# Shared experts first and a later routing step in two dense mixtures of a fused two-layer kernel

## The reference, cut to what matters

```python
shared = silu(h @ sWg) * (h @ sWu) @ sWd            # two shared experts' worth, width 256
routing_weights = sigmoid(h @ gate_w.T)             # 16 experts
topk_w, topk_idx = top_k(routing_weights, 8)
topk_w = topk_w / (sum(topk_w) + 1e-06) * 2.5
comb = zeros((T, 16)).at[arange(T)[:, None], topk_idx].add(topk_w)
eo[e] = (silu(h @ Wg[e]) * (h @ Wu[e])) @ Wd[e]     # every expert on every token
x = x + shared + sum_e eo[e] * comb[:, e]
```

## Time and profile before

| | |
|---|---|
| median of three runs | 1830.96 us |
| the profiled execution, its own time | 1826.19 us |
| its span, first to last instruction | 1824.3 us |
| PE busy | 1656.0 us, 91% |
| VectorE busy | 1331.1 us, 73% |
| ScalarE busy | 1009.8 us, 55% |
| GpSimd busy | 656.8 us, 36% |
| mean granted TensorE clock | 0.975 |
| HBM traffic over the span | 60 GB/s |

### The profile page before, as it was taken

The page is one execution under the profiler, slowest core; times in us unless marked ns, Lnnn a source line. Parts: engine busy times, 40 slices in busy tenths (PEclk is TensorE's granted clock), DMA queues, the critical chain, the costliest instruction groups (busy, mean ns, idle before and its releaser), DMA issues.

```text
span 1824.3 us, 34290 instructions
## 1 busy us (share of the span) xinstructions
PE 1656.0 (91%) x10911; PEld 1335.9 (73%) x10912; DVE 1331.1 (73%) x2842; ACT 1009.8 (55%) x2163; POOL 656.8 (36%) x604
## 2 busy tenths in 40 slices
PE   3877999899999999989999989899799999999998
PEld 1223888677777978777777779777588888887776
DVE  7997777778876577678778756665688888857664
ACT  4655543578786454348778744311588788744111
POOL 1664420266664042016566540100355555421000
PEclk8998999999999999999999999999899999999999
DMA  1000210000000122000000033398100010043695
GB/s 64 1 1 24 81 61 1 13 18 20 20 12 9 45 82 67 1 13 24 21 17 23 4 119 103 101 257 244 45 29 29 27 31 23 0 127 96 187 258 150
DMA packets 34895, 111.51 MB, mean 61 GB/s; under 512 B 4992, under 2 KB 18544, under 8 KB 27888
## 3 DMA queue, kind: packets, MB, share of 16 engines
q1 hardware_dynamic: 32424, 92.96, 16.8%
q10 hardware_dynamic: 2376, 17.30, 3.5%
HBM read 109.19 MB, written 1.05 MB: 60 GB/s over the span
## 4 chain that ended last, share of the span: by engine, by line
PE 65%; DVE 20%; ACT 8%; issue 6%; ACTq 1%; DMA 0%; DVEq 0%; POOL 0%; SPq 0%; POOLq 0%
PE banks L1046 8%; PE banks L1022 4%; PE banks L1762 4%; PE banks L1698 3%; PE banks L1001 3%; PE banks L594 3%; PE banks L596 3%; PE banks L595 3%; PE banks L1002 2%; PE banks L1003 2%; PE banks L953 2%; PE banks L1060 2%; PE banks L955 2%; PE banks L954 2%; PE banks L1061 2%
## 5 line engine op out<-in xcount | busy, mean ns | idle before, releaser
L1475 POOL TENSOR_TENSOR xn<-xn 128x512 f32<-128x512 f32 x132 | 171.4, 1299 | 247.5 <-DVE xn L1359 247.5
L1461 POOL TENSOR_SCALAR prob<-prob,recip 128x256 f32<-128x256 f32 (+2 forms) x256 | 228.5, 907 | 68.9 <-DVE recip L1343 68.8
L1230 ACT ACTIVATE prob<-banks,peak 128x256 f32<-128x256 f32 (+3 forms) x384 | 190.3, 501 | 107.7 <-DVE peak L1334 97.5
L1046 PE MATMUL banks<-pt,v 128*128 128x256 f32 (+3 forms) x768 | 203.2, 407 | 6.9 <-ACT pt L1165 6.9
L1046 PEld LDWEIGHTS banks<-pt,v 128*128 128x128 f32 x768 | 143.6, 189 | 73.5 <-issue 33.0
L1334 DVE TENSOR_REDUCE peak<-banks 128x1 f32<-128x256 f32 (+3 forms) x384 | 161.4, 448 | 16.6 <-PE banks L1005 15.2
L1001 PE MATMUL banks<-k_hi,q_hi 128*128 128x256 f32 (+2 forms) x384 | 152.2, 396 | 22.7 <-DVE k_lo L1350 22.4
L1446 POOL TENSOR_TENSOR wq_lo<-wq,wq_hi 128x256 fp32r<-128x256 f32 x48 | 35.7, 743 | 326.2 <-ACT wq_hi L1180 326.2
L1022 PE MATMUL banks<-ident,prob 128*128 128x128 f32 x864 | 140.6, 279 | 3.2 <-DVE pt L1163 3.2
L1359 DVE TENSOR_TENSOR xn<-xn,ropes 128x512 f32<-128x512 f32 x138 | 123.9, 898 | 0.0
L1002 PE MATMUL banks<-k_lo,q_hi 128*128 128x256 f32 (+2 forms) x384 | 120.4, 314 | 0.0
(11 more groups left out here) (255 smaller groups left out, 4988.2 us busy)
## 6 DMA issues: line engine op xcount, KB each, us to landing
wgu<-in_w_gu SPq DMA_DIRECT2D x32, 1408.0 KB, 15.0
wd<-in_w_d ACTq DMA_DIRECT2D x24, 704.0 KB
raw<-in_w SPq DMA_DIRECT2D x36, 384.0 KB, 3.1
wd<-in_w_d SPq DMA_DIRECT2D x8, 704.0 KB
wkv<-in_mha_kv SPq DMA_DIRECT2D x16, 256.0 KB, 2.6
wq<-in_mqa_q SPq DMA_DIRECT2D x16, 128.0 KB, 2.0
wo<-in_mqa_o SPq DMA_DIRECT2D x16, 128.0 KB, 2.1
wq<-in_gqa_q SPq DMA_DIRECT2D x16, 128.0 KB, 2.0
```

The costliest lines, as they stand in the source:

```text
L1046: last = pe.matmul(o_bank[:, x * P:to], v[:, s, x, at:at + P], pt[:, s, x, first:first + to - x * P], start=(j == 0), stop=(j == NQ - 1))
L1230: last = act.activation(prob[:, s, cols[t]:cols[t] + n], s_bank[gi][:, psum_col[t]:psum_col[t] + n], ACT.Exp, bias=peak[:, s, t:t + 1], ac ...
L1461: last = pool.tensor_scalar(part, part, recip[:, s, t:t + 1], None, ALU.mult)
L1475: pool.tensor_tensor(cosed_at(i, m, r), cosed_at(i, m, r), swap[:, r % 2, :], ALU.add) \
```

## The change

The expert that unit u computes is now `expert(u) = (u + 16) % 18`: the two shared experts come first, the routed ones behind. SP's loads and the column of the weights in `add` follow that order. `logits(0)` moves on PE from ahead of gate_up(0) to between gate_up(1) and down(0). DVE, after inner_low(0), waits for the logits and copies them raw from bank 6 to SBUF (count `shelved`); PE waits for that copy, not for the sigmoid, ahead of down(1). ACT's `gates(0)` now reads the copy in SBUF, in place, and moves behind inner_hi(1); the load of the sigmoid's table ahead of it is no longer written out, and a load of the silu's table follows it. `route(0)` moves on DVE from ahead of product(1) to behind add(1), ahead of product(3). The second sequence's logits, sigmoid and routing stay where they were. Both dense mixtures are built by the same function, so both change.

```diff
+    def expert(n):
+        return (n + NE0) % NU0
...
-            sp.dma_start(raw[:, n % 4, :], d["w0"][n]).then_inc(full[n % 4].sem, 16)
+            sp.dma_start(raw[:, n % 4, :], d["w0"][expert(n)]).then_inc(full[n % 4].sem, 16)
...
-        logits(0)
         norm.wait_parts(pe, 0)
         gate_up(0)
...
                 gate_up(u + 1)
+            if u == 0:
+                logits(0)
             if u == 1:
-                pe.wait_ge(c["gates"].sem, 1)
+                pe.wait_ge(c["shelved"].sem, 1)
...
         def gates(s):
-            act.wait_ge(c["logits"].sem, s + 1)
-            act.activation(score[:, s * HALF:(s + 1) * HALF, :].rearrange("p t e -> p (t e)"),
-                           g.banks[:, 6 - 2 * s, 0:HALF * NE0], ACT.Sigmoid).then_inc(c["gates"].sem, 1)
+            to = score[:, s * HALF:(s + 1) * HALF, :].rearrange("p t e -> p (t e)")
+            if s == 0:
+                act.wait_ge(c["shelved"].sem, 1)
+            else:
+                act.wait_ge(c["logits"].sem, s + 1)
+            act.activation(to, to if s == 0 else g.banks[:, 6 - 2 * s, 0:HALF * NE0], ACT.Sigmoid) \
+                .then_inc(c["gates"].sem, 1)
...
         norm.root(act, 1)
-        act.preload_act_table(ACT.Sigmoid)
-        gates(0)
         act.preload_act_table(ACT.Silu)
...
             act.activation(inner_hi[:, u % 2, :], inner[:, u % 2, :], ACT.Copy).then_inc(c["high"].sem, 1)
+            if u == 1:
+                gates(0)
+                act.preload_act_table(ACT.Silu)
...
-                last = dve.scalar_tensor_tensor(x, outs(u)[:, t, :], weight[:, s * HALF + t, n:n + 1], x,
+                last = dve.scalar_tensor_tensor(x, outs(u)[:, t, :], weight[:, s * HALF + t, expert(n):expert(n) + 1], x,
...
         inner_low(0)
-        route(0)
+        dve.wait_ge(c["logits"].sem, 1)
+        dve.tensor_copy(score[:, 0:HALF, :].rearrange("p t e -> p (t e)"), g.banks[:, 6, 0:HALF * NE0]) \
+            .then_inc(c["shelved"].sem, 1)
         for u in range(1, UNITS):
...
             add(u - 1)
+            if u == 2:
+                route(0)
```

More of the change, by code:

```diff
@@ L516, in mixture @@
     c = st.c = {n: st.count(n) for n in (
-        "loaded", "full_0", "full_1", "full_2", "full_3", "logits", "gates", "own", "w_high", "w_low",
+        "loaded", "shelved", "full_0", "full_1", "full_2", "full_3", "logits", "gates", "own", "w_high", "w_low",
         "inner", "silu", "prod", "high", "low", "down", "added")}
```

## The result

The changed kernel takes 1834.55 us, the median of 11 runs (1832.64 to 1837.6); the kernel before, on the same chip, 1830.21 us (11 runs, 1826.38 to 1832.88). The ratio is 1.0027, with a 95% interval of 1.0018 to 1.0035: 4.3 us slower. A second group of runs gave 1834.34 against 1829.38, ratio 1.0026 (1.0017 to 1.0035). The profiled execution of the changed kernel took 1837.6 us, the slowest of its runs, with a span of 1835.7; that of the kernel before was its fastest. So the 11.4 us between the two spans are not the effect of the change, and what follows compares stretches, not spans. The first dense mixture ends at about 342 us of the span of the kernel before, not at 326.

The account below looks back on a forecast made before the run. PE was taken as the bound, busy 1656.0 of 1824.3 us. Later down(3) starts (2.2 us) plus low clock behind two new waits (6.8 us) made 9.0 us slower: 1840.0 us on the median, range 1827 to 1847.

Parts of the forecast that it names:

- The front: First mixture up to down(0): gate_up(0) starts 1.6 us earlier, 1.7 us of logits eat it, down(0) does not move.
- The copy, the tables, the routing: DVE and ACT costs: copy 0.2 us plus 0.2 hand-over; two table loads and sigmoid 2.8; routing 2.53, at most 3.26.
- Down(3): Unit 3 of both mixtures: starts 1.9 us later in the first, 0.25 in the second, each behind a 3.6 us PE wait.
- it fell after all seven: In the old trace the clock fell after each of seven PE waits of 3.4 to 5.8 us begun at full clock.
- the class that always fell: PE waits of 3.4 to 5.8 us, after which the clock dropped; both new 3.6 us waits were put there.
- a loss of 3.4 us each: Behind each mixture's wait at unit 3: 6.8 us at half speed, bounds 1.7 and 5.1, in all 6.8 us lost.
- the likeliest case: Clock falls behind the unit 3 wait in both mixtures: 1836 to 1843 us, chance 0.40.
- yardstick of 5.5 us: Whole kernel: a measurement can tell 0.3%, 5.5 us; slower by more 0.50, same 0.36, faster 0.14.
- signs of being wrong: At unit 3: forecast wrong if the wait is under 2 us or the clock stays at 1.00 behind it.
- (A): Waits at unit 3 come, but clock holds or falls in one mixture only, briefly: 1833 to 1836.4 us, chance 0.33.
- (B): Longer waits at unit 3, routing collides in both mixtures, low spells cost 5.1 us each: 1844.9 us, chance 0.15.
- (C): Faster: shift behind the mixtures removes five low spells elsewhere and the new waits are spared: 1824.7 us, chance 0.12.

Follow-up runs that it names:

- route_only: Kernel before with only the experts' order changed and route(0) moved behind add(1), front left as before, no copy: 1834.31 us against 1829.22, ratio 1.0032.
- fill_wait: Changed kernel with gate_up(4) issued twice in each dense mixture, the first without a semaphore: 1831.36 us against the changed kernel's 1834.34; ratio to before 1.0014.
- look_2: Changed kernel unaltered, run again for one more trace to count clock falls behind the waits at unit 3: 1834.99 us.
- route_unit1: Changed kernel with route(0) moved one unit forward on VectorE, behind add(0) and ahead of product(2): 1830.67 us, ratio 1.0007 to the kernel before.

## Why the prediction was right in kind and too large in size

- **The front.** It said gate_up(0) starts 1.6 us earlier and the logits eat that. So it was, but for the clock: the prediction let it rise 6.0 us after the dense matmuls began, and it rose 5.0 us after (174.54 to 179.50), which is within the 1 us that its bounds left for this. All eleven traces with the logits moved have a low stretch of 10.2 us at the front; the three with the logits there (twice before, and route_only) have 13.7.
- **The copy, the tables, the routing.** 0.23 us for the copy (0.2 assumed). From hi(1) on, table, sigmoid and table took 2.8 us as predicted. The routing took 2.53 us, free of GpSimd. product(3) to down(3) was 4.94 and 4.95, against the 4.94 before.
- **Down(3).** +1.26 us in the first mixture against the 1.9 predicted (product(2) came 15.55 us behind gate_up(0), not 16.1, mostly since the clock rose earlier), +0.18 in the second against 0.25. Waits of 3.24 and 3.43 us against 3.6. These steps held, and fill_wait and route_only show that they belong to the routing's place.
- **The term that was mis-sized** is "it fell after all seven ... The two new waits of 3.6 us are in the class that always fell ... a loss of 3.4 us each". The cost of one fall was right or low: read from down(3) to down(7), the six cost 3.2 us twice, 4.2, 4.3, and 4.7 twice. But a fall came behind 6 of 10 waits, not all. Most of them were also outside the class: the shortest of its seven waits was 3.40 us, the predicted new ones were 3.6, and the real ones came out at 3.23 to 3.43. In the medians, the falls and all that the shift does elsewhere come to about 3 us, not 6.8: 4.3 to 5.0 us of slowdown less 1.4 of path, and 3.0 us between the changed kernel and fill_wait. The six falls of the five traces would make more, 24.3 / 5 = 4.9 us a run. With the path that is 6.3 us, just inside the measured interval of the slowdown (3.3 to 6.4 us), so the difference of some 2 us may be noise or fewer low spells elsewhere; five traces are too few to tell.
- **The forecast as a whole.** 1834.55 us is inside the range of 1827 to 1847, a wide one, but below the 1836 to 1843 of the likeliest case (both fall, 0.40). By the prediction's own yardstick of 5.5 us, the 4.3 us are "same", to which it gave 0.36, against 0.50 for slower. The direction is clear of noise all the same (1.0018 to 1.0035). Of its signs of being wrong, a wait under 2 us did not come; a clock that stays at 1.00 behind the wait came four times in ten.
- **The rivals.** (A), that the clock holds, or falls in one mixture only, describes the typical run: in four of five traces it fell once, and the time lies in its 1833 to 1836.4, though the falls were of 6.8 or 10.2 us and not brief. It had a chance of 0.33. (B) did not come. (C) did not come for the change; but that low spells elsewhere differ by several from run to run, on which it rested, is true, and is the reason that a profile's own span told nothing of 4 us.
- **The skill's rule.** The Trainium skill ("TensorE: Matmul & The Clock Gate", HAM oscillation) names idle gaps of PE of a certain length as what drops the clock. These runs do not agree that length alone decides: 3.42 us without a fall (look_2, second mixture), 2.48 with one (route_only).

## What to carry to other kernels

Ask of moved work what its new neighbours are: the routing took VectorE 2.5 us and more wherever it stood, but behind add(1) it stood just ahead of the one unit whose wait already ran through the same engine (xt, xh, xl), and two modest delays made one wait of 3.3 us. Keep such work apart by a unit or two, or cut it to fit the idle places; here either turned 4 us lost into 4 us won. And where a change makes one long wait of PE out of several short ones, price the clock behind it as a chance, not as a certainty.

## What the runs showed of the hardware that was not expected

- Small DVE instructions can be held until a GpSimd instruction ends. In route_unit1, L727 (128x4, SBUF to SBUF) took 1.81 us from 191.09 to 192.90 while GpSimd's tensor_tensor ran from 191.03 to 192.87, and 1.81 again in the second mixture; without that it takes 0.17. In the kernel before, L715 took 0.95 us from 643.66 to 644.61 while GpSimd's ran from 642.68 to 644.52; without that it takes 0.23. The Trainium skill ("GPSIMD Engine Reference", Specifications) names contention on the shared SBUF interfaces for two kinds of DVE instructions, those with two SBUF inputs and those in a two-port mode. L715, which has two SBUF inputs, agrees; whether L727, which has one, ran in such a mode is in no row.
- The low stretch at the front of the first mixture lasted 13.7 us in the three traces in which PE did the 16 small matmuls of the logits (3.6 us) ahead of gate_up(0), and 10.2 us in the eleven in which gate_up(0) came there, 1.6 us earlier. What in this brings the clock back sooner was not separated.
- The same program's low time varied from 87 to 110 us between the five traces of the changed kernel, and its span from 1825.7 to 1835.7.
